# A two-layer transformer on one core: the maxima, totals, sums and biases around a feed-forward step are placed anew

## The chip, the cores and the metric

The kernel runs on one core of one Trainium2 chip. Its engines each work through a stream of their own: TensorE (PE in the profile; its weight loads are PEld), VectorE (DVE), ScalarE (ACT), GpSimd (POOL) and SyncE (SP), which here only issues DMAs. The metric is device time in microseconds (us) from the first to the last instruction of the core, median of several runs; less is better.

## The reference

Two transformer layers run one after the other over four sequences of 1024 tokens of width 512. Cut to what matters:

```python
# layer 0, 16 heads of 32, rotary positions
h = layer_norm(x) * (1 + scale1) + shift1          # shift, scale from cond
q, k, v = h @ wq + bq, h @ wk + bk, h @ wv + bv
q, k = rotary(q), rotary(k)
x = x + softmax(q @ k.T / sqrt(32) masked) @ v @ wo + bo
h = layer_norm(x) * (1 + scale2) + shift2
x = x + gelu(h @ ff_w1 + ff_b1) @ ff_w2 + ff_b2    # 512 -> 2048 -> 512
# layer 1: 16 query heads on 4 key/value heads, no positions, no mask
h = ln(x) * (1 + sc1) + sh1
x = x + g1 * (softmax(q @ k.T / sqrt(32)) @ v @ wo.T)
h = ln(x) * (1 + sc2) + sh2
x = x + g2 * (gelu(h @ w1.T + b1) @ w2.T + b2)
```

The result is float32. The kernel keeps it so by writing each operand of a product as a high and a low float16 half, and making three float16 products of the halves.

## The kernel before

**Images.** The work is eight images, `i` = 0 to 7: the four sequences of layer 0 (`i` = 0 to 3), then those of layer 1 (4 to 7). An image is an attention stage and a feed-forward stage. Every engine has an `attention(i)` and a `forward(i)`, written out by hand in one order, so each engine is a queue: a wait holds all that stands behind it. Semaphores (`Count` objects) link the queues.

**Attention.** It has 64 steps `s`. In each, TensorE makes four score tiles (128 keys x 512 queries, `score`, L946) into three PSUM banks in turn. ScalarE takes the exponential of each (`exps`, L1125) into `probs`, six units of two tiles in turn. TensorE multiplies a unit pair with the values (`values`, L963, bank 4). GpSimd adds two units (`add_probs`, L692) into `sums`, which TensorE multiplies by ones for the softmax denominators (`totals`, L978, bank 5): 64 additions `m`, and 32 totals, one for each pair of additions. A unit of `probs` is used again only when both its product and its addition are done. The eight last additions alternate between GpSimd and VectorE (`by_vector`: m = 57, 59, 61, 63).

Row maxima are needed before the exponential. For the next block of four heads TensorE makes scores a second time, with queries on the partitions (`max_item`, L884), and VectorE reduces each tile to a column (`tensor_reduce`, L1443). These tiles, and all other narrow work ("keys": projections `q`, `k`, `v`; output projection `wo`; transposes `ln1`, `ln2` of the normalised rows), go through three PSUM banks in attention and two (6 and 7) in the feed-forward stage; `bank_free` waits until the bank's reader is done. `fills_of` and `narrow_forward` say at which step which key stands. `wo` tiles 0 to 3 stand at steps 54 to 57 (`WO_AT`), their normalisation (`norm_apply`, L1343) right behind tile 3, the transposes at 61 and 62 (`LN2_AT`). Then come the last total, the feed-forward stage, and ScalarE's copies of bank 4 and 5 (`o_copy`, `d_copy`), VectorE's reciprocal of the last denominators (`invert_last`, L1460) and GpSimd's product of the two (`normalise`).

In layer 0 `k` and `q` are turned (rotary): VectorE makes four products in `turn`, GpSimd joins them (`rotate`, L677), ScalarE takes the high half, GpSimd the low half (`stack_low`, L682), SyncE puts them into the stack `ks` by six DMAs (`put_stack`, L518). `TURNS` holds the additions m behind which GpSimd does this. In images 0 to 3 weights are also split into halves (`split_low`, L1491), 18 chunks in image 0 and 7 each in images 1 to 3.

**Feed-forward.** Steps `n` = 0 to 32. At step n TensorE makes the first product of hidden chunk n (12 matmuls, L783 to L785 with `aT,ring`, into bank 4 or 5), then the second product of chunk n-1 (12 matmuls, three for each of four row tiles, `ring,probs`, banks 0 to 3), then the keys of that step. ScalarE takes the Gelu of chunk n into `g32` (L1271), VectorE splits it into halves (`split`, L1534 and L1535) and then drains the keys. Chunks 0 to 15 belong to the first 512 tokens, 16 to 31 to the others. At the end of each half VectorE reads the four row tiles (`output`, L1548 in layer 0, L1544 in layer 1). In layer 1 a second addition follows (`output_sum`, L1553). Keys of a feed-forward stage are the `wo` tiles 4 to 7 (n = 2, 3), transposes (n = 4 to 9), the next image's projections (n = 10 to 21), and its first 32 maxima, four each at n = 21 and 22 and three each at n = 23 to 30.

**GpSimd between them.** Behind the last addition it makes three deviations (L670, L672: reciprocal roots for normalisation) and adds the bias of the second product to all eight row tiles (`add_last_bias`, L711).

```python
                    for key in narrow_forward(i, n):      # TensorE, end of a forward step
                        narrow(key)
```

## Time and profile before

| | |
|---|---|
| median of 3 runs | 4138.36 us (4135.44 to 4140.47) |
| the profiled execution | 4144.66 us, its span 4142.9 us |
| TensorE busy | 3823.0 us, 92% |
| VectorE busy | 2498.1 us, 60% |
| GpSimd busy | 1626.7 us, 39% |
| ScalarE busy | 1605.7 us, 39% |
| granted TensorE clock, mean | 0.968 |

A layer-0 image takes some 537 us, a layer-1 image some 478 us, and images of a layer are alike almost to 0.1 us, step by step. So one image can be read closely and multiplied. Since all queues are in a fixed order, the question at each place is which wait of TensorE ends last, and what the engine that ends it did before.

### The profile page before, as it was taken

The numbers are of one execution on the slowest core, as the hardware profiler recorded it, in microseconds if no ns is written. First come the engines' busy times: TensorE is split into PE (matmuls) and PEld (weight loads), VectorE is DVE, ScalarE is ACT, GpSimd is POOL, SyncE is SP. The second block draws the span as 40 slices with busy tenths as digits, with TensorE's granted clock in tenths as the row PEclk, the third lists the DMA queues.
The fourth block names the chain that finished last, engine by engine and source line by source line (L and its number), as shares of the span: only waits on it lengthen the run. The fifth ranks groups of instructions, "written<-read, shape, count | busy, mean of one in ns | idle before, by whom it ended". The sixth has DMA issues, their size and how long they took to land.

```text
span 4142.9 us, 53495 instructions
## 1 busy us (share of the span) xinstructions
PE 3823.0 (92%) x20400; PEld 1511.9 (36%) x20400; DVE 2498.1 (60%) x3944; ACT 1605.7 (39%) x2807; POOL 1626.7 (39%) x907
## 2 busy tenths in 40 slices
PE   6898998998998989889899998999899998989999
PEld 4322443233533334333343333433244333433244
DVE  4687635767356764466654777367664776457752
ACT  1366312553125631155421663136521563126621
POOL 2377212673116742066510673026510573106620
PEclk9899999999999999999999999999999999999999
DMA  5233242221422223332222021311222112311112
GB/s 147 43 105 115 73 109 68 81 58 64 105 72 77 58 80 86 90 77 60 87 95 89 14 70 60 109 37 27 80 72 94 29 37 77 105 56 24 60 63 93
DMA packets 138973, 305.21 MB, mean 74 GB/s; under 512 B 19632, under 2 KB 59588, under 8 KB 137824
## 3 DMA queue, kind: packets, MB, share of 16 engines
q10 hardware_dynamic: 50944, 174.62, 13.0%
q1 hardware_dynamic: 87776, 127.17, 11.8%
q8 instruction: 164, 2.69, 0.3%
q14 instruction: 89, 0.73, 0.1%
HBM read 223.46 MB, written 36.66 MB: 63 GB/s over the span
## 4 chain that ended last, share of the span: by engine, by line
PE 76%; DVE 13%; issue 4%; POOL 3%; ACT 2%; DMA 1%; SPq 0%; ACTq 0%; DVEq 0%; POOLq 0%
PE ps L783 11%; PE ps L785 11%; PE ps L784 11%; PE ps L963 10%; PE ps L884 9%; PE ps L946 8%; PE ps L820 7%; PE ps L978 5%; DVE mcol L1443 3%; PE ps L837 2%; ACT probs L1125 2%; DVE turn L1365 1%; POOL sums L692 1%; DVE v_sb L1343 1%; PE ps L801 1%
## 5 line engine op out<-in xcount | busy, mean ns | idle before, releaser
L692 POOL TENSOR_TENSOR sums<-probs 128x1024 f32<-128x1024 f32 x480 | 1137.2, 2384 | 1393.0 <-ACT probs L1125 849.8
L1443 DVE TENSOR_REDUCE mcol<-ps 128x1 f32<-128x512 f32 x2048 | 1281.0, 683 | 368.5 <-PE ps L884 365.8
L1125 ACT ACTIVATE probs<-ps 128x512 f32<-128x512 f32 x2048 | 1100.5, 606 | 852.5 <-PE ps L946 625.9
L884 PE MATMUL ps<-ks,qs 97*128 97x512 f16 x2048 | 796.3, 395 | 126.2 <-DVE mcol L1443 76.0
L946 PE MATMUL ps<-qs,ks 98*128 98x512 f16 x2048 | 780.2, 392 | 78.0 <-ACT probs L1125 76.1
L1271 ACT ACTIVATE sums<-ps,cols 128x512 f32<-128x512 f32 x256 | 175.9, 687 | 1185.5 <-PE ps L785 1185.5
L963 PE MATMUL ps<-probs,v_sb 128*32 128x512 f32 x4096 | 560.1, 621 | 0.0
L884 PEld LDWEIGHTS ps<-ks,qs 97*128 97x128 f16 x2048 | 202.4, 99 | 708.2 <-DVE mcol L1443 436.1
L1534 DVE CAST probs<-sums 128x512 f16<-128x512 f32 x256 | 129.8, 507 | 485.7 <-ACT sums L1271 485.4
L783 PE MATMUL ps<-aT,ring 128*128 128x512 f16 x1024 | 395.2, 386 | 0.0
L784 PE MATMUL ps<-aT,ring 128*128 128x512 f16 x1024 | 394.0, 385 | 0.0
L785 PE MATMUL ps<-aT,ring 128*128 128x512 f16 x1024 | 393.7, 385 | 0.0
L783 PE MATMUL ps<-ring,probs 128*128 128x512 f16 x1024 | 388.6, 379 | 2.6 <-DVE probs L1535 2.5
L784 PE MATMUL ps<-ring,probs 128*128 128x512 f16 x1024 | 388.5, 379 | 0.0
L785 PE MATMUL ps<-ring,probs 128*128 128x512 f16 x1024 | 388.5, 379 | 0.0
L946 PEld LDWEIGHTS ps<-qs,ks 98*128 98x128 f16 x2048 | 198.8, 99 | 376.3 <-ACT probs L1125 245.8
L820 PE MATMUL ps<-hT,wqkv 128*128 128x512 f16 x1248 | 300.6, 386 | 4.8 <-DVE wqkv L1610 4.8
L978 PE MATMUL ps<-sums,ones 128*32 128x512 f32 x2048 | 277.6, 615 | 19.5 <-DVE sums L1436 19.5
L677 POOL TENSOR_TENSOR turn<-turn 128x512 f32<-128x512 f32 x32 | 41.6, 1299 | 610.4 <-DVE turn L1379 610.4
L1535 DVE TENSOR_TENSOR probs<-sums,probs 128x512 f16<-128x512 f32 x256 | 189.2, 739 | 8.8
L1379 DVE SCALAR_TENSOR_TENSOR turn<-ps,bias,trig 128x512 f32<-128x512 f32 x128 | 89.9, 746 | 166.5 <-PE ps L820 150.1
L820 PEld LDWEIGHTS ps<-hT,wqkv 128*128 128x128 f16 x1248 | 121.5, 99 | 164.3 <-issue 14.5
(107 smaller groups left out, 3286.5 us busy)
## 6 DMA issues: line engine op xcount, KB each, us to landing
ring<-halves ACTq DMA_DIRECT2D x208, 512.0 KB, 3.4
qs<-hl SPq DMA_DIRECT2D x192, 128.0 KB, 4.0
ring<-halves SPq DMA_DIRECT2D x48, 512.0 KB, 6.2
ring<-in_weights ACTq DMA_DIRECT2D x39, 512.0 KB, 4.3
halves<-ring ACTq DMA_DIRECT2D x37, 512.0 KB, 2.9
ks<-hl SPq DMA_DIRECT2D x120, 128.0 KB, 4.3
dcopy<-inverses SPq DMA_DIRECT2D x56, 256.0 KB
probs<-in_x SPq DMA_DIRECT2D x8, 1024.0 KB, 7.2
```

What stands on the lines that cost most here:

```text
L692: pool.tensor_tensor(sums[:, m % SUM_SLOTS, :, :], prob(u - 2), prob(u), ALU.add).then_inc(sum_set[0].sem, 1)
L783: pe.matmul(dst, lhs[0], rhs[0], start=first, stop=False)
L784: pe.matmul(dst, lhs[0], rhs[1], start=False, stop=False)
L785: return pe.matmul(dst, lhs[1], rhs[0], start=False, stop=last)
L820: mm = pe.matmul(bank, qkv(lw, weight_at(kind, i, hh, part, c), P), hT[:, lx, c, tok], start=(q == 0), stop=(q == 11))
L884: pe.matmul(bank, qs[0:K_MAX, hh, h, P * qt:P * qt + P], ks[0:K_MAX, key_set(i, hh), key_head(i, hh, h), 512 * half:512 * half + 512], sta ...
L946: pe.matmul(ps[:, bank, :], ks[0:K_EXP, key_set(i, hh), key_head(i, hh, h), P * kt:P * kt + P], qs[0:K_EXP, hh, h, :], start=True, stop=Tr ...
L963: mm = pe.matmul(ps[32 * q:32 * q + 32, 4, :], values_of(i, hh)[:, kt, value_cut(i, hh, 4 * g + q)], prob(u + q // 2)[:, q % 2, :], start= ...
L978: mm = pe.matmul(ps[32 * q:32 * q + 32, 5, :], ones32[:, :], sums[:, (m + q // 2) % SUM_SLOTS, q % 2, :], start=(m % 8 == 0), stop=(m % 8 ...
L1125: act.activation(prob(u)[:, e, :], ps[:, w % SCORE_BANKS, :], ACT.Exp).then_inc(exp_done.sem, 1)
L1443: dve.tensor_reduce(mcol[:, blk % 2, 4 * j + qt, half:half + 1], src, AX.X, ALU.max).then_inc(n_free[0], 1)
L1535: dve.tensor_tensor(fT[:, n % 4, 1, :], g32[:, n % 2, :], fT[:, n % 4, 0, :], ALU.subtract).then_inc(f_set.sem, 1)
```

## The change

- `forward` of TensorE: where a step's keys begin with a maximum and are more than two (`spread`), the first stands behind the first product, the second behind the second row tile of the second product, the rest at the end. VectorE takes the first maximum ahead of `split`.
- `totals`: the pair before the last comes one step later (behind the last `values`), the last pair behind the first product of the feed-forward stage. `d_copy(i, 7)` follows the first Gelu. `g32` moves to another slot of `sums`, so that the first Gelu waits for one total less. In layer 0 the first two pairs come one step earlier.
- `by_vector`: additions 57 and 59 go to GpSimd. `WO_AT`, `LN2_AT` are 2 less, `BIAS_AT` is earlier, the deviation stands at m = 53. `TURNS` of the second `k` half: low half at m = 3, high half at unit 10, its stack DMAs at step 6 ahead of the row DMA.
- `add_last_bias` waits until VectorE has applied the last normalisation of the next image.
- `output_sum` goes from VectorE to GpSimd: row tiles 0 to 3 behind the biases and builds, 4 to 7 behind additions 0 to 3 of the next image.
- `output` waits for each row tile by a new semaphore `y_full`, not for the whole product.
- `norm_apply` subtracts and multiplies in one instruction for each tile; the small instruction L1336 (`nm`) is gone.
- `split_low` is cut into two halves, at steps st and st+1.

```diff
-LAG, LAG_D = 4, 6
+LAG = 4
-WO_AT = 54
-LN2_AT = 61
-BIAS_AT = (50, 51, 52, 53, 54, 55, 56, 58)
+WO_AT = 52
+LN2_AT = 59
+BIAS_AT = (49, 49, 50, 51, 53, 54, 55, 56)
-("k", 1, 1), 3, 4, 11
+("k", 1, 1), 3, 3, 10
...
+def totals_step(i, pair):
+    return 2 * pair + (3 if layer(i) == 0 and pair < 2 else 4)
 def by_vector(m):
-    return m >= SUMS - 8 and m % 2 == 1
+    return m in (SUMS - 3, SUMS - 1)
+def spread(keys):
+    return len(keys) > 2 and keys[0][0] == "max"
...
             def output_sum(i, tt):                            # GpSimd
+                pool.wait_ge(y_read.sem, y_read.at(i, tt + 1))
+                pool.tensor_tensor(x1(i)[:, tt, :], x1(i)[:, tt, :], turn[:, tt % 4, :], ALU.add).then_inc(y_set.sem, 1)
...
+                    if gated(i - 1) and m < 4:
+                        output_sum(i - 1, 4 + m)
...
+                if i + 1 < NB:
+                    pool.wait_ge(ln_n, NORMS["ln1", i + 1, 1] + 1)
                 add_last_bias(i, 0)
...
-                    m = sum_of(max(u - LAG_D, 0))
-                    if u >= LAG_D and u - LAG_D == sum_unit(m):
-                        totals(i, m)
+                    if s == STEPS + 1:
+                        totals(i, SUMS - 4)
+                    for pair in range(SUMS // 2 - 2):
+                        if s == totals_step(i, pair):
+                            totals(i, 2 * pair)
...
                         mm.then_inc(f1_mm.sem, 1)
+                    if n == 0:
+                        totals(i, SUMS - 2)
+                    keys = narrow_forward(i, n)
+                    some(keys[0:1] if spread(keys) else ())
...
+                            if g == FC - 1 and t < 3:
+                                mm.then_inc(y_full.sem, 1)
+                            if t == 1:
+                                some(keys[1:2] if spread(keys) else ())
                         mm.then_inc(f2_mm.sem, 1)
-                    for key in narrow_forward(i, n):
-                        narrow(key)
+                    some(keys[2:] if spread(keys) else keys)
...
-                link(dve.scalar_tensor_tensor(out=nm[:, :], in0=mv[:, :, 0], scalar=-1.0, in1=rs[:, :],
-                                              op0=ALU.mult, op1=ALU.mult))
...
-                    last = dve.tensor_scalar(dst[:, t, :], src, rs[:, t:t + 1], nm[:, t:t + 1], ALU.mult, ALU.add)
+                    last = dve.tensor_scalar(dst[:, t, :], src, mv[:, t, 0:1], rs[:, t:t + 1], ALU.subtract, ALU.mult)
...
             def output(i, th):
-                dve.wait_ge(f2_mm.sem, f2_mm.at(i, FC * (th + 1)))
                 dve.wait_ge(xy_set.sem, xy_set.at(i, 4 * th + 4))
...
+                    if t < 3:
+                        dve.wait_ge(y_full.sem, y_full.at(i, 3 * th + t + 1))
+                    else:
+                        dve.wait_ge(f2_mm.sem, f2_mm.at(i, FC * (th + 1)))
...
                 for n in range(2 * FC + 1):
+                    keys = narrow_forward(i, n)
+                    for key in keys[0:1] if spread(keys) else ():
+                        narrow(key)
                     if n < 2 * FC:
                         split(i, n)
```

TensorE's order in image 0, from the last scores into the first product, before (L963 values, L978 totals, L783 to L785 the first product):

```order
L963 MATMUL ps<-probs,v_sb 32x512 x4
L978 MATMUL ps<-sums,ones 32x512 x4
L946 MATMUL ps<-qs,ks 128x512 x4
L963 MATMUL ps<-probs,v_sb 32x512 x8
L978 MATMUL ps<-sums,ones 32x512 x4
L963 MATMUL ps<-probs,v_sb 32x512 x4
L978 MATMUL ps<-sums,ones 32x512 x4
L783 MATMUL ps<-aT,ring 128x512
```

And now, where values are L986, totals L1001 and the first product L806 to L808 (its twelve matmuls are shown from the first and up to the last):

```order
L1001 MATMUL ps<-sums,ones 32x512 x4
L969 MATMUL ps<-qs,ks 128x512 x4
L986 MATMUL ps<-probs,v_sb 32x512 x12
L1001 MATMUL ps<-sums,ones 32x512 x4
L806 MATMUL ps<-aT,ring 128x512
...
L808 MATMUL ps<-aT,ring 128x512
L1001 MATMUL ps<-sums,ones 32x512 x4
L806 MATMUL ps<-aT,ring 128x512
```

The last total has moved behind the first product, and the one before it behind all values.

TensorE's order at the end of forward step 23 before: the second product's last row tile, three maxima (L884), and the next step:

```order
L783 MATMUL ps<-ring,probs 128x512
L784 MATMUL ps<-ring,probs 128x512
L785 MATMUL ps<-ring,probs 128x512
L884 MATMUL ps<-ks,qs 128x512 x3
L783 MATMUL ps<-aT,ring 128x512
```

The same stretch now (maxima L907):

```order
L808 MATMUL ps<-aT,ring 128x512
L907 MATMUL ps<-ks,qs 128x512
L806 MATMUL ps<-ring,probs 128x512
L807 MATMUL ps<-ring,probs 128x512
L808 MATMUL ps<-ring,probs 128x512
L806 MATMUL ps<-ring,probs 128x512
L807 MATMUL ps<-ring,probs 128x512
L808 MATMUL ps<-ring,probs 128x512
L907 MATMUL ps<-ks,qs 128x512
```

Each maximum now has six or more other matmuls between it and the next.

GpSimd's order in the same image, before, from the deviation at m = 55 to the biases between the stages (additions L692, bias L700, normalise L719, low half L725):

```order
L670 TENSOR_TENSOR sd<-mv,eps 128x4 [waits ln_var]
L672 TENSOR_TENSOR rs<-sd,eps 128x4 [waits sd_set]
L692 TENSOR_TENSOR sums<-probs 128x1024 [waits d_mul,exp_done]
L700 TENSOR_TENSOR ks<-ks,row_bc 128x512
L725 TENSOR_TENSOR aT<-ocopy,aT 128x512 [waits at_hi]
L692 TENSOR_TENSOR sums<-probs 128x1024 [waits d_mul,exp_done]
L700 TENSOR_TENSOR ks<-ks,row_bc 128x512
L692 TENSOR_TENSOR sums<-probs 128x1024 [waits d_mul,exp_done] x2
```

And now from the deviation at m = 53 (additions L702, bias L710, normalise L734, low half L740):

```order
L682 TENSOR_TENSOR rs<-sd,eps 128x4 [waits sd_set]
L702 TENSOR_TENSOR sums<-probs 128x1024 [waits d_mul,exp_done]
L710 TENSOR_TENSOR ks<-ks,row_bc 128x512
L734 TENSOR_TENSOR ocopy<-ocopy,dcopy 128x512 [waits inv_set,o_out]
L702 TENSOR_TENSOR sums<-probs 128x1024 [waits d_mul,exp_done]
L710 TENSOR_TENSOR ks<-ks,row_bc 128x512
L702 TENSOR_TENSOR sums<-probs 128x1024 [waits d_mul,exp_done]
L710 TENSOR_TENSOR ks<-ks,row_bc 128x512
L702 TENSOR_TENSOR sums<-probs 128x1024 [waits d_mul,exp_done]
L740 TENSOR_TENSOR aT<-ocopy,aT 128x512 [waits at_hi]
L702 TENSOR_TENSOR sums<-probs 128x1024 [waits d_mul,exp_done] x4
```

Behind the deviation GpSimd has eight additions where it had four.

## Rows read from the trace of the kernel before

**Rows 1.** Windows: stretch, its length, busy us per engine, granted clock, DMA share, GB/s.
```profile
1147.83:1200.43 52.60, 48.04 (x217) 20.88 (x216) 24.05 (x41) 5.50 (x8) 0.00 (x0) 1.00 0.15 50
4085.86:4127.30 41.44, 41.44 (x193) 18.75 (x192) 8.96 (x16) 5.50 (x8) 0.00 (x0) 1.00 0.20 68
1000.76:1018.92 18.16, 18.16 (x98) 9.75 (x97) 16.14 (x34) 5.19 (x8) 5.59 (x7) 1.00 0.27 87
1018.92:1038.87 19.95, 14.79 (x66) 7.45 (x64) 16.27 (x19) 4.37 (x7) 8.26 (x6) 0.83 0.15 53
910.51:977.45 66.94, 55.61 (x326) 18.33 (x324) 40.39 (x49) 35.49 (x64) 39.87 (x25) 0.95 0.23 82
3415.41:3482.98 67.57, 56.17 (x326) 18.44 (x324) 43.20 (x53) 34.63 (x63) 31.16 (x18) 0.95 0.24 84
2272.89:2290.75 17.86, 17.86 (x89) 5.08 (x88) 15.68 (x26) 12.97 (x24) 9.85 (x5) 0.90 0.24 75
2748.03:2770.05 22.02, 19.63 (x89) 5.49 (x88) 20.65 (x30) 13.38 (x24) 10.30 (x5) 0.85 0.24 72
```

**Rows 2.** TensorE's timeline, forward step 23: start, us, work [idle before, releaser].
```profile
1154.18 0.39 PE L884 MATMUL ps<-ks,qs 97*128 97x512 f16 x1 [0.57 <-DVE mcol L1443]
```

**Rows 3.** Timelines of GpSimd, VectorE and TensorE, forward steps 6 and 7, image 1.
```profile
1015.71 11.46 POOL L711 TENSOR_TENSOR ks<-ks,row_bc 128x512 f32<-128x512 f32 x8
...
1017.45 1.49 DVE L1534 CAST probs<-sums 128x512 f16<-128x512 f32 x1
...
1021.80 5.67 DVE L1343 TENSOR_SCALAR probs<-probs,rs,nm 128x512 f32<-128x512 f32 x4
...
1030.27 0.42 DVE L1534 CAST probs<-sums 128x512 f16<-128x512 f32 x1
...
1029.06 1.09 PE L801 MATMUL ps<-ident,v_sb 128*128 128x128 f32 x4 [4.79 <-DVE aT L1366]
```

**Rows 4.** Timelines of VectorE, TensorE and GpSimd, attention steps 58 to 60, image 1.
```profile
940.40 2.33 DVE L1336 SCALAR_TENSOR_TENSOR nm<-mv,rs 128x4 f32<-128x4 f32 x1 [1.41 <-POOL rs L672]
942.77 6.63 DVE L1343 TENSOR_SCALAR v_sb<-ks,rs,nm 128x512 f32<-128x512 f32 x4
949.33 1.21 DVE L1436 TENSOR_TENSOR sums<-probs 128x1024 f32<-128x1024 f32 x1
...
951.31 1.58 PE L946 MATMUL ps<-qs,ks 98*128 98x512 f16 x3 [6.12 <-ACT probs L1125]
...
942.67 1.27 POOL L700 TENSOR_TENSOR ks<-ks,row_bc 128x512 f32<-128x512 f32 x1
```

**Rows 5.** Timelines of TensorE, ScalarE and VectorE, end of attention, image 1.
```profile
971.26 1.07 PE L978 MATMUL ps<-sums,ones 128*32 128x512 f32 x8 [2.44 <-DVE sums L1436]
...
972.38 0.60 ACT L1137 ACTIVATE dcopy<-ps 128x512 f32<-128x512 f32 x1 [2.90 <-PE ps L978]
...
973.01 3.35 DVE L1460 RECIPROCAL dcopy<-dcopy 128x512 f32<-128x512 f32 x1 [1.90 <-ACT dcopy L1137]
```

**Rows 6.** Timelines of VectorE and TensorE, end of image 1's feed-forward stage.
```profile
1209.28 2.48 DVE L1548 SCALAR_TENSOR_TENSOR ks<-ps,ks 128x512 f32<-128x512 f32 x4 [1.85 <-PE ps L785]
...
1211.91 0.59 PE L884 MATMUL ps<-ks,qs 97*128 97x512 f16 x1 [2.23 <-DVE ks L1548]
```

**Rows 7.** VectorE's timeline, attention step 3, image 5.
```profile
2758.37 0.68 DVE L1553 TENSOR_TENSOR ks<-ks,turn 128x512 f32<-128x512 f32 x1
```

**Rows 8.** Timelines of GpSimd and TensorE, attention steps 5 to 8, image 2.
```profile
1242.55 2.35 POOL L692 TENSOR_TENSOR sums<-probs 128x1024 f32<-128x1024 f32 x1 [6.32 <-PE ps L978]
...
1261.21 0.58 PE L884 MATMUL ps<-ks,qs 97*128 97x512 f16 x1 [4.97 <-DMA ks<-hl]
```

**Rows 9.** VectorE's timeline, step 21, image 2; then line L1491: min/median/max ns.
```profile
1324.61 3.17 DVE L1491 SCALAR_TENSOR_TENSOR ring<-ring 128x1024 f16<-128x1024 f32 x1
...
L1491 DVE SCALAR_TENSOR_TENSOR ring<-ring x37: 1149/1224/3169, 190.7 to 1860.8; 128x1024 f16<-128x1024 f32 x37
```

**Rows 10.** GpSimd's timeline, steps 21 and 22, image 2: two additions.
```profile
1322.02 4.67 POOL L692 TENSOR_TENSOR sums<-probs 128x1024 f32<-128x1024 f32 x2 [1.23 <-PE ps L978]
```

More of the change, by code:

```diff
@@ L360, in program @@
         f2_mm = count("f2_mm", 2 * FC)
+        y_full = count("y_full", 6)
         exp_done = count("exp_done", SCORES)
@@ L733, in attention @@
                         add_probs(i, m)
-                    if layer(i) == 0 and m in BIAS_AT:
-                        add_bias(i, BIAS_AT.index(m))
-                    if m == 55:
+                    for tt, at_ in enumerate(BIAS_AT):
+                        if layer(i) == 0 and m == at_:
+                            add_bias(i, tt)
+                    if m == 53:
                         deviation("ln2", i, 0)
@@ L776, in _ @@
                     first_builds(i + 1)
+                if gated(i):
+                    for tt in range(4 if i + 1 < NB else NT):
+                        output_sum(i, tt)
         @block.tensor
@@ L982, in attention @@
             def attention(i):
-                for s in range(STEPS + LAG_D // 2):
+                for s in range(STEPS + LAG // 2):
                     u = 2 * s
@@ L1252, in attention @@
                 o_copy(i, 7)
-                d_copy(i, 7)
             def narrow(key):
@@ L1568, in forward @@
                             norm_apply("ln1", j, n // 6)
-                    for key in narrow_forward(i, n):
+                    for key in keys[1:] if spread(keys) else keys:
                         narrow(key)
```

42 lines of the change are left out of this document (22 added, 20 removed).

## Prediction

> **What bounds the kernel.** TensorE is busy 92% of the span, so it is the bound and only its waits and idle stretches can be gained. I read the timeline of one image of each layer step by step, noted where a step is longer than its matmuls, and put windows around those places [rows 1]. Feed-forward: in the last image, which has no next image's maxima, eight steps of 24 matmuls take 41.44 us, 0.216 us a matmul; in the others the same eight steps with three maxima each take 52.60. The 24 maxima themselves are 5.2, so 6.0 us are waits, three quarters of a microsecond a step: the third maximum waits until VectorE has read the first, as only two banks serve them [rows 2]. Steps 7 and 8 take 19.95 us where steps 4 to 6 take 6.05 each: GpSimd adds eight biases, VectorE's ops beside them stretch, and TensorE waits 4.79 us for a bank [rows 3]. The end of attention (from step 52 to the first matmul of the second product) takes 66.94 us in layer 0 and 67.57 in layer 1 [rows 1]; in it TensorE waits 6.12 us because VectorE is held in a normalisation ahead of addition 57 [rows 4], and 2.44 us for addition 63 [rows 5].
>
> The granted clock shows 0.83 and 0.95 in these windows against 1.00 around them: TensorE runs on its half level (1.2 of 2.4 GHz) for some us after such an idle stretch. So a removed wait can give back more than itself.
>
> **Part 1, spread maxima.** Now the first product, half a second product and the other half lie between maxima, 1.3 us or more, and VectorE takes the first maximum before Gelu is ready. Its work in a step, three maxima and two split ops, is half of the step (24.05 us of 52.60 [rows 1]), and the split is due a whole product later. So the waits go: 6.0 us for steps 23 to 30, and another 0.75 for step 22. Step 21 begins with a maximum only where the next image is of layer 1, 0.75 more in four of seven stages. 7 x 6.75 + 4 x 0.75 = **50 us**. Bounds: 4.6 us a stage (eight waits of 0.57 [rows 2]), so 32; and 55, if four maxima waited longer than three.
>
> **Part 2, biases behind the normalisation.** Steps 7 and 8 are 7.85 us over 2 x 6.05. The cast that takes 1.49 us beside GpSimd takes 0.42 alone [rows 3], a tensor op of the split's size 0.68 [rows 7]. So from 1017.45 on VectorE needs 0.42 + 0.7 for the split and, at the cast's length (an estimate), four times 0.46 for the applications, and is through near 1020.4 instead of 1027.5. Then GpSimd starts its eight biases, 1.27 each [rows 4], near 1020.5 to 1031, beside five VectorE ops on SBUF that each wait for one. Walking it through, TensorE waits 0.3 + 0.7 + 0.9 + 0.7 + 0.3 = 2.9 us in steps 7 to 9. Gain 7.85 - 2.9 = 5.0, seven times: **35 us**. Bounds: nothing (the same eight biases stand in another place) and 7.85 each, 55.
>
> How the two engines stand in each other's way is shown by one split op: it begins at 1324.61, takes 3.17 us where the median is 1.22 [rows 9], and GpSimd's second of two additions ran until 1326.69 [rows 10]. The op waits for the whole rest of that addition.
>
> The Trainium skill says this of the pair: one SBUF port pair is shared, whoever starts first keeps it for a whole instruction (SBUF — State Buffer, "SBUF: two separate sides"). The trace agrees, as above. It also advises against elementwise work on GpSimd, at about twice VectorE's time (GPSIMD Engine Reference, "4.1 Engine selection"); the trace agrees here too, 1.27 [rows 4] against 0.68 [rows 7]. By that rule parts 3 and 5 are steps in the wrong direction; what they do here is worked out in their own terms.
>
> **Part 3, end of attention.** VectorE no longer has addition 57 behind its normalisation (6.63 us [rows 4], where the small op ahead of it, 2.33, goes as well). But GpSimd now has: behind the deviation, additions 54 to 60 (7 x 2.34 [rows 10]), biases 3 x 1.27, and two ops of a bias's size: 23 us for layer 0, 19 for layer 1 (no biases there), and the exponentials of the last units wait for them. The `wo` tiles, 2.6 us each, move into steps 52 and 53 and out of 56 and 57, where they lengthen the stage no more. The walk, for image 1: step 56 begins at 933.7 (910.5 plus four steps of 6.3, 5.4, 6.9, 4.6), the deviation is done 1.9 later, addition 54 at 938, 55 at 943 (a bias and a normalise between), 57 at 950, 59 at 957, each on an exponential's path; unit 123 ends near 959, the total of step 62 and addition 61 near 963.4, the last two exponentials, the last values and bank 4's copy near 966.2. There the first product starts. In layer 1, without biases, the same walk ends 3.1 sooner. That is 6.1 us earlier in layer 0 (972.3 before) and 9.2 in layer 1. Some is given back: the last total now follows the first product (2.6 us), and behind it stand, as before, the copy of 0.60, the reciprocal of 3.35 [rows 5] and the split of 1.1 [rows 3, 7], for which the second product waits. So that starts 8.9 us behind the first, not 5.2 to 6. Net 2.4 in layer 0, 6.3 in layer 1: 4 x 8.7 = **35 us**. The copy cannot be late for the first product, as bank 4's copy runs under the last pair's total. Bounds: -3.7 an image (only the give-back; -30) and +7 in layer 0, +9 in layer 1 (GpSimd never late; 64).
>
> **Part 4, output by row tiles.** The four reads take 2.48 us, all behind the product, and TensorE idles 2.23 [rows 6]. Now three of them run under the product's last tiles, as far as VectorE has drained the two maxima before: 1.8 us earlier, seven times, **13 us**, and about 1 at the kernel's end, where the last sums, though slower on GpSimd, start sooner. Bounds 5 and 20 (the half clock at the next image's start gone too).
>
> **Part 5, output sums on GpSimd.** Images 5 to 7 spend 22.02 us on steps 0 to 5 where image 4, without output sums, takes 17.86 [rows 1]. GpSimd's pair of 2.34 + 1.27 = 3.6 us a step for four steps is above the 3 us of a step there, so I give back half: 3 x 2.1 = **6 us**. Bounds -6 (queue never catches up) and 12.5.
>
> **Part 6, the second key half of layer 0.** Addition 3 waits 6.32 us for the first total, and TensorE 4.97 for the stack's DMAs three steps later [rows 8]. With totals one step earlier and the low half right behind the turn, the six DMAs go out some 5 us sooner. I count 4.5 of the wait, and 1.5 of the half clock behind it: 4 x 6 = **24 us**. The row DMA is now queued behind the six on SyncE; it is needed a step later, and if late takes 2 us of this back. Bounds 10 and 28.
>
> **Part 7, halved split op.** 39 of them. GpSimd's pairs of additions fill the odd steps, so one half of each now falls into a free step and one into a busy one. Those that cost 3.17 cost about 2.6 and 0.6, and those that were free (1.22 in even steps) now meet an addition: **0**. Bounds -20 and +15.
>
> **The sum.** 50 + 35 + 35 + 13 + 1 + 6 + 24 + 0 = 164 us. The profiled execution took 4144.7 and would take 3980.7; the median is 6.3 below it, so 3974 us.
>
> **Rivals.**
> *Contention pays it back.* GpSimd is queued wherever work was taken from VectorE: parts 2 and 3 come to nothing. For it: 23 us of GpSimd work in a row on the path. Against: those waits had VectorE behind GpSimd twice over. 4144.7 - 94 - 6.3 = 4044. Chance 0.13.
> *Maxima not freed.* The first maximum now stands ahead of the split on VectorE and the spread ones meet its ops, so the wait moves to the second product: part 1 gives nothing, 4024. Against it speaks VectorE's half-empty step. Chance 0.05.
> *Everything clears, the clock too.* All upper bounds but part 7's: 55 + 55 + 64 + 21 + 12 + 28 = 235, so 3903. For it: each wait is tied to a stretch at half clock, and a shorter chain tends to unlock the next. Chance 0.16.
> *Slower: the halved splits.* Twice as many VectorE ops meet an addition of up to 2.34 us while holding the maxima, and ScalarE, which stores the split and is in order, now waits for the later half. If each of 39 costs 5 us, 195 are lost: 4144.7 - 164 + 195 - 6.3 = 4169. It decides from 4.2 us a split; today's worst step loses about that, but only seven splits meet it. Chance 0.02.
>
> **How the numbers follow.** The forecast has the remaining 0.64; its own range from the bounds is 3930 to 4030. Most of the second case and of the clearing one must be within: low 3925, high 4045. 0.2% is about what a measurement of this kernel can tell from no change. Only the last rival is slower: 0.02; within 0.2% 0.01; faster 0.97.
>
> **What would show it.** Forward steps 23 to 30 in 46.6 us; steps 7 and 8 near 15 without an idle stretch of 4 us; no wait above 1 us for the stack's DMAs at attention step 7; TensorE's idle before the next image's first maximum below 0.7; between first and second product near 9 us, with the reciprocal as the last releaser. If GpSimd is the releaser of long waits of ScalarE in steps 56 to 60, part 3 was right in kind. A wait of the second product for the split in steps 22 to 30, or of ScalarE's queue for the halved split, would prove me wrong.

## The result, and the profile after

The changed kernel takes 4037.31 us (median of four runs, 4033.12 to 4039.97); the kernel before, on the same chip, 4139.41 (also of four). One run of the kernel before, 4235.98 us, lies apart in a slower state and is left out of the ratio, whose other three runs have a median of 4138.36. The ratio is 0.9755, 95% interval 0.9738 to 0.9772. So it is faster, by 102 us where 164 were forecast; 4037 lies inside the range 3925 to 4045, near its upper end. The profiled execution's span is 4038.1 us against 4142.9, so the two traces hold the whole difference.

Windows of the changed kernel, with the columns of [rows 1] and in the same order of places:

```profile
1128.80:1175.53 46.73, 46.73 (x218) 21.05 (x216) 24.65 (x41) 5.50 (x8) 0.00 (x0) 1.00 0.19 62
3982.41:4023.85 41.44, 41.44 (x193) 18.78 (x192) 8.96 (x16) 5.50 (x8) 0.00 (x0) 1.00 0.20 67
990.70:1008.86 18.16, 18.16 (x98) 9.77 (x97) 15.95 (x36) 5.19 (x8) 2.41 (x4) 1.00 0.26 87
1008.86:1020.96 12.10, 12.10 (x66) 6.51 (x64) 11.93 (x14) 4.26 (x7) 10.80 (x7) 1.00 0.27 88
893.97:965.76 71.79, 59.35 (x325) 18.93 (x324) 37.05 (x47) 36.77 (x66) 46.44 (x28) 0.90 0.23 82
3320.89:3393.74 72.85, 60.34 (x326) 18.59 (x324) 41.13 (x51) 35.42 (x64) 36.68 (x20) 0.91 0.22 80
2210.93:2228.36 17.43, 16.91 (x90) 4.68 (x89) 15.46 (x26) 12.95 (x24) 9.86 (x5) 1.00 0.31 76
2672.31:2690.00 17.69, 17.10 (x89) 4.52 (x88) 15.45 (x26) 12.49 (x23) 12.83 (x7) 1.00 0.21 75
```

Read against [rows 1], line by line: the eight forward steps with maxima fall from 52.60 to 46.73, steps 7 and 8 from 19.95 to 12.10, and in both TensorE is now busy without a gap. Steps 0 to 5 of image 5 fall from 22.02 to 17.69. But the end of attention became longer: from step 52 to the second product 71.79 us and not 66.94 in image 1, 72.85 and not 67.57 in image 6, at a granted clock of 0.90 and not 0.95.

I cut both traces at the same matmuls and summed over the eight images. This is the table that the rest is about (us saved, minus is lost):

| stretch | part | forecast | measured |
|---|---|---|---|
| forward steps 21 to 30 | 1, spread maxima | 50 | 53.4 |
| forward steps 7 to 9 | 2, biases later | 35 | 56.8 |
| attention step 52 to first product | 3, end of attention | | -7.7 |
| first to second product | 3, last total | | -31.1 |
| second product to forward step 4 | 3 | | -6.5 |
| all of part 3 | 3 | 35 | -45.3 |
| end of the second product to the next image, and kernel's end | 4, output by tile | 14 | 14.3 |
| attention steps 0 to 6 | 5, output sums | 6 | 10.0 |
| attention steps 7 and 8 | 6, second key half | 24 | 30.0 |
| attention steps 9 to 51 | 7, halved split | 0 | -15.0 |

With 0.3 from forward steps 4 to 6 the sum is 104.5, of a difference of 104.8 between the spans.

The places where it went well, in the changed kernel's timelines (VectorE, TensorE and GpSimd of image 1) and in one line of TensorE's waits:

```profile
1008.17 1.91 DVE L1374 TENSOR_SCALAR probs<-probs,mv,rs 128x512 f32<-128x512 f32 x4
...
1013.58 1.49 DVE L1571 CAST probs<-sums 128x512 f16<-128x512 f32 x1
...
1182.51 2.56 DVE L1590 SCALAR_TENSOR_TENSOR ks<-ps,ks 128x512 f32<-128x512 f32 x4
...
1185.21 0.38 PE L907 MATMUL ps<-ks,qs 97*128 97x512 f16 x1 [0.44 <-DVE ks L1590]
...
1010.16 12.47 POOL L721 TENSOR_TENSOR ks<-ks,row_bc 128x512 f32<-128x512 f32 x8 [4.48 <-DVE probs L1374]
...
PE ps L907 <- DMA ks<-hl: 0.3, 1, 0.3
```

The application of the norm takes 1.91 us for four tiles where it took 5.67 beside GpSimd [rows 3], and the eight biases begin only behind it. TensorE's wait for the last output is 0.44, not 2.23 [rows 6], and of the waits for the stack's DMAs (4.97 in [rows 8]) 0.3 us is left in the whole kernel.

Where it went badly, GpSimd, VectorE and TensorE of the changed kernel at steps 56 to 61 of image 6:

```profile
3346.99 0.20 POOL L680 TENSOR_TENSOR sd<-mv,eps 128x4 f32<-128x4 f32 x1 [4.50 <-DVE mv L1364]
...
3348.26 2.35 POOL L702 TENSOR_TENSOR sums<-probs 128x1024 f32<-128x1024 f32 x1
...
3351.98 5.01 POOL L702 TENSOR_TENSOR sums<-probs 128x1024 f32<-128x1024 f32 x2
3361.10 2.36 POOL L702 TENSOR_TENSOR sums<-probs 128x1024 f32<-128x1024 f32 x1 [4.10 <-PE ps L1001]
...
3364.53 2.35 POOL L702 TENSOR_TENSOR sums<-probs 128x1024 f32<-128x1024 f32 x1
3372.36 4.97 POOL L702 TENSOR_TENSOR sums<-probs 128x1024 f32<-128x1024 f32 x2 [5.49 <-PE ps L1001]
...
3348.32 8.96 DVE L1374 TENSOR_SCALAR v_sb<-ks,mv,rs 128x512 f32<-128x512 f32 x4 [1.41 <-POOL rs L682]
...
3367.57 0.63 PE L824 MATMUL ps<-ident,v_sb 128*128 128x128 f32 x4 [2.38 <-DVE aT L1397]
```

These additions are m = 54, then 55 and 56, 57, 58, then 59 and 60. GpSimd first waits 4.50 us for VectorE's statistics, with addition 54 queued behind. Then VectorE's four applications take 8.96 us beside its additions (1.91 above, alone). Additions 57 and 59 wait 4.10 and 5.49 us for totals: only three slots hold sums, so an addition needs the total of the one three before it, and that total stands in TensorE's queue behind score tiles, values and transposes.

And between the two products, VectorE and TensorE of the same image:

```profile
3388.38 3.35 DVE L1493 RECIPROCAL dcopy<-dcopy 128x512 f32<-128x512 f32 x1 [3.03 <-ACT dcopy L1169]
...
3392.05 1.64 DVE L1572 TENSOR_TENSOR probs<-sums,probs 128x512 f16<-128x512 f32 x1
...
3388.49 0.38 PE L806 MATMUL ps<-aT,ring 128*128 128x512 f16 x1 [0.81 <-ACT dcopy L1169]
3393.74 0.39 PE L806 MATMUL ps<-ring,probs 128*128 128x512 f16 x1 [2.50 <-DVE probs L1572]
```

The second product begins 9.8 us behind the first, waiting for the split, which waits for the reciprocal, which waits for the copy of the last total.

### The profile page after: what moved, and what is told of

Read it like the earlier page. It is cut to its first block, busy times and chain, and to the rows that moved or that the text cites. A ratio compares the mean times of both kernels' runs of the same rounds, so it can differ in the third digit from the quotient of the medians.

```text
span 4038.1 us, 53506 instructions
## 1 busy us (share of the span) xinstructions
PE 3800.2 (94%) x20400; PEld 1502.4 (37%) x20400; DVE 2466.3 (61%) x3903; ACT 1603.3 (40%) x2807; POOL 1711.6 (42%) x955
## 4 chain that ended last, share of the span: by engine, by line
PE 80%; DVE 9%; POOL 4%; issue 3%; ACT 3%; DMA 1%; SPq 0%; ACTq 0%; POOLq 0%; DVEq 0%
PE ps L806 12%; PE ps L807 12%; PE ps L808 12%; PE ps L986 10%; PE ps L907 9%; PE ps L969 8%; PE ps L843 7%; PE ps L1001 5%; DVE mcol L1476 3%; PE ps L860 2%; POOL sums L702 2%; ACT probs L1157 2%; DVE ring L1526 2%; PE ps L824 1%; DVE dcopy L1493 1%
## 5 line engine op out<-in xcount | busy, mean ns | idle before, releaser
L702 POOL TENSOR_TENSOR sums<-probs 128x1024 f32<-128x1024 f32 x496 | 1175.6, 2384 | 1039.5 <-PE ps L1001 570.0
L907 PE MATMUL ps<-ks,qs 97*128 97x512 f16 x2048 | 790.6, 388 | 64.4 <-DVE mcol L1476 47.0
L986 PE MATMUL ps<-probs,v_sb 128*32 128x512 f32 x4096 | 568.0, 631 | 0.0
L907 PEld LDWEIGHTS ps<-ks,qs 97*128 97x128 f16 x2048 | 199.7, 98 | 624.9 <-DVE mcol L1476 375.2
L806 PE MATMUL ps<-ring,probs 128*128 128x512 f16 x1024 | 390.8, 382 | 20.6 <-DVE probs L1572 20.6
L806 PE MATMUL ps<-aT,ring 128*128 128x512 f16 x1024 | 388.3, 379 | 6.5 <-ACT dcopy L1169 6.5
L808 PE MATMUL ps<-ring,probs 128*128 128x512 f16 x1024 | 389.9, 381 | 0.0
L807 PE MATMUL ps<-aT,ring 128*128 128x512 f16 x1024 | 388.2, 379 | 0.0
L808 PE MATMUL ps<-aT,ring 128*128 128x512 f16 x1024 | 388.0, 379 | 0.0
L1001 PE MATMUL ps<-sums,ones 128*32 128x512 f32 x2048 | 280.6, 621 | 0.0
L1572 DVE TENSOR_TENSOR probs<-sums,probs 128x512 f16<-128x512 f32 x256 | 207.4, 810 | 8.8
```

The source lines that it names most:

```text
L702: pool.tensor_tensor(sums[:, m % SUM_SLOTS, :, :], prob(u - 2), prob(u), ALU.add).then_inc(sum_set[0].sem, 1)
L806: pe.matmul(dst, lhs[0], rhs[0], start=first, stop=False)
L807: pe.matmul(dst, lhs[0], rhs[1], start=False, stop=False)
L808: return pe.matmul(dst, lhs[1], rhs[0], start=False, stop=last)
L907: pe.matmul(bank, qs[0:K_MAX, hh, h, P * qt:P * qt + P], ks[0:K_MAX, key_set(i, hh), key_head(i, hh, h), 512 * half:512 * half + 512], sta ...
L986: mm = pe.matmul(ps[32 * q:32 * q + 32, 4, :], values_of(i, hh)[:, kt, value_cut(i, hh, 4 * g + q)], prob(u + q // 2)[:, q % 2, :], start= ...
```

## The experiments

Each kernel is the changed one, or the one before, with the edit shown. Differences "by the traces" are from the same cuts as in the table. The runs are from several chips, so each ratio is to the kernel before as measured beside that run, and kernels are best compared by their ratios.

### Transposes back to steps 61 and 62 (r_ln2)

```diff
-LN2_AT = 59
+LN2_AT = 61
```

> The changed kernel, LN2_AT back to 61: the transposes of the second normalisation stand at steps 61 and 62 again, all else stays. In the changed kernel TensorE waits 2.5 us at step 60 for VectorE's low half of the first pair of transposes, and its totals, which free the slots of the sums, stand behind them; GpSimd's next addition waits 6.4 us (image 1) and 8.3 us (image 6) for such a total. Theory A (TensorE's order: the earlier transposes are what ate the gain): the stall of step 60 goes, the stretch from step 52 to the first product becomes 4 to 6 us shorter in each of eight images, 4037 - 32 to 48 = 3989 to 4005. Theory B (GpSimd's queue, longer by additions 57 and 59, is what ate it): this edit changes less than 1 us an image, 4029 to 4045. A transposition that then stands right ahead of the first product may cost up to 2 us an image under either.

Measured: 4039.92 us, ratio 0.9752 (0.9737 to 0.9766), the same as the changed kernel. Step 60 of image 6 falls from 7.98 to 3.65 us as theory A wanted, but step 62 grows from 4.43 to 7.37 and step 63 from 4.99 to 6.25. TensorE, GpSimd and VectorE of this kernel there:

```profile
3372.07 1.09 PE L824 MATMUL ps<-ident,v_sb 128*128 128x128 f32 x4 [1.60 <-DVE aT L1397]
...
3378.07 2.37 POOL L702 TENSOR_TENSOR sums<-probs 128x1024 f32<-128x1024 f32 x1 [6.88 <-ACT probs L1157]
...
3378.67 2.32 DVE L1397 TENSOR_TENSOR aT<-turn,aT 128x512 f16<-128x512 f32 x1
```

The wait goes with the transposes. Over eight images the stretch to the first product is 6.2 us shorter, and 3.2 of it are lost behind. Theory A falls as the cause. Theory B is left standing, without being shown yet.

### Additions 57 and 59 back on VectorE (r_vec)

```diff
-    return m in (SUMS - 3, SUMS - 1)
+    return m >= SUMS - 8 and m % 2 == 1
```

> The changed kernel, by_vector as before: additions 57, 59, 61, 63 on VectorE. Theory B (GpSimd's queue ate the gain): step 52 to the first product becomes 3 to 6 us shorter an image, 3989 to 4013. Theory A (TensorE's order): VectorE's norm_lo ops now have two more additions of 1.2 us beside them and the first of them stands behind the normalisation again, 0 to 3 us longer an image, 4037 to 4061.

Measured: 4014.67 us, ratio 0.9693 (0.9677 to 0.9709). The stretch to the first product is 31.1 us shorter by the traces, 2.9 to 4.5 in each image, 3.9 on average, where theory B asked 3 to 6. The whole kernel gains less, some 23 us, and so ends 2 us above theory B's 4013: 5.5 us are lost in steps 9 to 51, which the edit doesn't touch, and 1.7 behind the second product. Theory B holds for the stretch, at its lower end. VectorE, GpSimd and TensorE in steps 59 to 61 of image 6 (additions 57 to 60):

```profile
3343.20 1.23 DVE L1469 TENSOR_TENSOR sums<-probs 128x1024 f32<-128x1024 f32 x1 [3.78 <-PE ps L1001]
...
3351.52 1.23 DVE L1469 TENSOR_TENSOR sums<-probs 128x1024 f32<-128x1024 f32 x1 [1.75 <-PE ps L1001]
...
3345.29 2.36 POOL L702 TENSOR_TENSOR sums<-probs 128x1024 f32<-128x1024 f32 x1 [3.18 <-ACT probs L1157]
...
3352.90 2.36 POOL L702 TENSOR_TENSOR sums<-probs 128x1024 f32<-128x1024 f32 x1 [5.25 <-ACT probs L1157]
...
3348.47 0.63 PE L824 MATMUL ps<-ident,v_sb 128*128 128x128 f32 x4 [0.93 <-DVE aT L1397]
```

Both additions that go back take 1.23 us and not 2.36, and 59 and 60 no longer stand in a row (4.97). The feared loss, that the first of them would again stand behind the normalisation, isn't there: the normalisation was over before addition 57's slot was free. GpSimd now waits for exponentials, and not they for it. What this run can't separate is the longer addition itself from its meetings with VectorE's low halves of the transposes. The one that takes 1.61 us in the changed kernel takes 0.69 here, but a later one takes 2.30.

### The last total in front of the first product (r_total)

```diff
-                    if n == 0:
-                        totals(i, SUMS - 2)
...
+                totals(i, SUMS - 2)
...
                 o_copy(i, 7)
+                d_copy(i, 7)
...
-                    if n == 0:
-                        d_copy(i, 7)
```

On TensorE the last total stands behind the last step of attention, on ScalarE its copy behind that of bank 4.

> The changed kernel with the last pair's total in front of the first product of the feed-forward stage again, and the copy of bank 5 ahead of the first Gelu, as in the kernel before. Theory C1 (the total costs what it delays: copy, reciprocal and split run beside the first product again, but TensorE waits for addition 63, 1.4 us, and makes the total, 1.0, before it): first product 2.6 us later, second product 5.8 behind it and not 9.8, net 1.4 us an image, 4037 - 11 = 4026. Theory C2 (my prediction's reading: the whole give-back of 3.7 us an image is the price of the move): 4037 - 30 = 4007. If the move had been a gain, the time is above 4040.

Measured: 4024.76 us, ratio 0.9713 (0.9697 to 0.9729). Its span is 4023.5 us, 14.6 less than the changed kernel's. The first product comes later by 17.3 us in sum, the second follows it 32.4 sooner, and 6.5 more come from a stretch that is at half clock in four images of the changed kernel. TensorE waits 1.51 us for addition 63, as C1 said, and 0.65 for the split:

```profile
3375.57 1.06 PE L1001 MATMUL ps<-sums,ones 128*32 128x512 f32 x8 [1.51 <-DVE sums L1467]
...
3382.57 0.39 PE L806 MATMUL ps<-ring,probs 128*128 128x512 f16 x1 [0.65 <-DVE probs L1570]
```

These three make 21.5; 7.1 of it are lost again in steps 9 to 51 of the layer-0 images, which the edit doesn't touch. So moving the total costs some 15 us net in this order of work, up to 21 if that loss is chance: C1, above its 11. The 31 us between the products are not its price; 17 of them are bought back by the earlier first product.

### The reciprocal behind the first split (r_recip)

```diff
-                invert_last(i)
...
                 dve.wait_ge(gelu_done.sem, gelu_done.at(i, n + 1))
+                if n == 0:
+                    dve.wait_ge(*sum_done(SUMS - 2, i))
...
+                    if n == 0:
+                        invert_last(i)
```

All on VectorE: `invert_last` goes from the end of `attention` to behind `split(i, 0)`. The new wait for addition 62 takes over what the reciprocal's own wait had covered: the split writes where that addition reads.

> The changed kernel, with VectorE's last reciprocal (3.35 us) behind the first split of the feed-forward stage, not ahead of it. Theory C (the give-back of some 4 us an image between first and second product is the chain last total, copy, reciprocal, split, which now begins behind the first product): the second product starts near 5.3 us behind the first, not 9.8, so 8 x 4.5 = 36 us less, 4001. If the wait were for the Gelu or its table load (1.28 us) instead, 9.8 would fall to 8 or more and the time to 4023 at best. The reciprocal could delay the second split; it has about 5 us to the third product.

Measured: 4016.67 us, ratio 0.9695 (0.968 to 0.9709). The second product starts 7.1 us behind the first (21.6 us in sum) and the half-clock stretch behind it is gone (6.5). VectorE and TensorE, image 6:

```profile
3370.01 0.69 DVE L1573 TENSOR_TENSOR probs<-sums,probs 128x512 f16<-128x512 f32 x1
3370.62 3.34 DVE L1493 RECIPROCAL dcopy<-dcopy 128x512 f32<-128x512 f32 x1
...
3370.59 0.38 PE L806 MATMUL ps<-aT,ring 128*128 128x512 f16 x1 [0.81 <-ACT dcopy L1169]
```

Theory C is right in kind, its size (4001) wasn't: I had left out TensorE's own queue. Between the two products stand the total (1.04), the wait of 0.81 for its copy and another first product (2.6), so 7.1 and not 5.3 is the floor.

### The weight split in one piece (r_split)

```diff
                         if s == st:
-                            split_low(i, q, 0)
-                        if s == st + 1:
-                            split_low(i, q, 1)
+                            split_low(i, q)
```

`split_low` is again the one op of 1024 elements of the kernel before.

> The changed kernel with the weight split in one piece again (39 ops instead of 78). The stage sums of the two traces put the loss of steps 9 to 52 at 15 us; theory D (the halves cause it): 4037 - 15 = 4022, steps 9 to 24 and 24 to 52 as in the kernel before. Rival: the loss comes from the totals that stand two units earlier in TensorE's order there, and the halves cost nothing: 4037 within 3.

Measured: 4018.06 us, ratio 0.9695 (0.9679 to 0.9712), 20.2 us by the traces: theory D, and more than it asked. The line of the split op in the changed kernel (min/median/max ns, first and last start), then the same in this kernel, then a half in the changed kernel's timeline of VectorE:

```profile
L1526 DVE SCALAR_TENSOR_TENSOR ring<-ring x74: 615/780/2752, 184.2 to 1815.4; 128x512 f16<-128x512 f32 x74
```

```profile
L1524 DVE SCALAR_TENSOR_TENSOR ring<-ring x37: 1149/1226/3164, 183.7 to 1788.7; 128x1024 f16<-128x1024 f32 x37
```

```profile
771.86 2.63 DVE L1526 SCALAR_TENSOR_TENSOR ring<-ring 128x512 f16<-128x512 f32 x1
```

A half that meets an addition takes 2.63 us, nearly as long as a whole (3.16). Together the halves keep VectorE busy for 98.0 us and the whole ones for 65.3: the same lines grouped by form show this.

```profile
L1526 DVE SCALAR_TENSOR_TENSOR ring<-ring 128x512 f16<-128x512 f32 x74 | 98.0, 1327 | 4.8 <-ACT ring L1183 4.8
```

```profile
L1524 DVE SCALAR_TENSOR_TENSOR ring<-ring 128x1024 f16<-128x1024 f32 x37 | 65.3, 1764 | 4.8 <-ACT ring L1183 4.8
```

VectorE's longer busy time is not yet a loss; the loss is where somebody waits. ScalarE issues the DMA that stores each split, in its own queue, two steps behind the first half, and the second half now stands one step later. One line of ScalarE's waits in the changed kernel (us in total, times, longest), and VectorE and ScalarE of image 0 at steps 56 and 57:

```profile
ACT probs L1157 <- DVE ring L1526: 24.4, 9, 10.5
```

```profile
399.11 7.85 DVE L1374 TENSOR_SCALAR v_sb<-ks,mv,rs 128x512 f32<-128x512 f32 x4 [1.41 <-POOL rs L682]
406.88 1.75 DVE L1526 SCALAR_TENSOR_TENSOR ring<-ring 128x512 f16<-128x512 f32 x1
...
409.11 3.05 ACT L1157 ACTIVATE probs<-ps 128x512 f32<-128x512 f32 x6 [10.46 <-DVE ring L1526]
```

Here the second half stands behind the normalisation on VectorE, and the exponentials behind the store on ScalarE, for 10.46 us. Neither the kernel before nor this one has any such wait. Six of the nine, 19.0 us, are in image 0, which has 18 of the 39 splits; 15.2 of the 15.8 us that this run gains in steps 9 to 51 are in image 0 too. Whether two short ops at one place, with the store where it was, would cost anything was not tried.

### The kernel before with the spread maxima alone (p_spread)

The edit is the lines with `spread` of the diff above, on TensorE and VectorE.

> The kernel before with the spread maxima alone (the order of the keys on TensorE and VectorE, nothing else). If the waits of steps 21 to 30 are that order's alone: step 21 to the end of step 30 shortens by 53 us over seven stages, 4139 - 53 = 4086. If the rest of the change had a part in it (outputs by tile, sums on GpSimd), less than 45, above 4094.

Measured: 4089.32 us, ratio 0.987 (0.9855 to 0.9885). Forward steps 21 to 30 are 53.4 us shorter (41.2 and 12.3), as in the changed kernel to a tenth, the other stretches of the images give 1 us back, and the start ahead of the first attention stage is 2 us shorter. Part 1 stands by itself.

### The kernel before with the later biases alone (p_bias)

```diff
                     deviation("ln1", i + 1, 1)
+                    pool.wait_ge(ln_n, NORMS["ln1", i + 1, 1] + 1)
                 add_last_bias(i, 0)
```

> The kernel before with one wait more: GpSimd adds the last biases only when VectorE has applied the next image's second normalisation. If their meeting was the whole cost of steps 7 and 8: 57 us over seven stages, 4139 - 57 = 4082, each of steps 7 to 9 in 6.05. If the shorter application of the changed kernel (one small instruction less, two scalars from one pair) had a part in it, up to 16 us of that stay missing: 4098.

Measured: 4092.87 us, ratio 0.9877 (0.9862 to 0.9892). Forward steps 7 to 9 are 56.5 us shorter; the attention stages give back 4. So the order of the two engines there was the whole cost, and the shorter application of the changed kernel had no part in it: one wait in one queue is worth 52 us.

### The kernel before with only the earlier places at the end of attention (p_end)

```diff
-WO_AT = 54
-LN2_AT = 61
-BIAS_AT = (50, 51, 52, 53, 54, 55, 56, 58)
+WO_AT = 52
+LN2_AT = 59
+BIAS_AT = (49, 49, 50, 51, 53, 54, 55, 56)
...
-                    if m == 55:
+                    if m == 53:
                         deviation("ln2", i, 0)
```

> The kernel before with only the earlier places at the end of attention: wo tiles at 52, transposes at 59, biases from 49, deviation at 53; additions and totals stay. In the runs of the changed kernel the placing is bound up with the totals (worth some 17 us there in that stretch, taken back behind it) and with additions 57 and 59 (-31). Theory E (the placing is worth nearly nothing, because the chain of deviation, additions, normalisation and transposes moves with it): step 52 to the first product shortens by 6 us over eight images, within 10 of it, 4139 - 6 = 4133. My prediction's reading (the placing is the gain, 6 to 9 us an image): 50 to 70 us, 4070 to 4090.

Measured: 4149.14 us, ratio 1.0008 (0.9998 to 1.0018): nothing. By the traces the first product comes earlier, by 17.3 us in sum (3.2 an image in layer 0, 1.1 in layer 1), and 18.6 and 7.1 are lost behind it. (The trace is of the fastest of ten runs; it also has 8.4 us less in steps 9 to 51, which the edit doesn't touch, and so its span is 4 us under the kernel before's.) GpSimd, ScalarE, VectorE and TensorE around the second product of image 6:

```profile
3465.01 1.26 POOL L719 TENSOR_TENSOR ocopy<-ocopy,dcopy 128x512 f32<-128x512 f32 x1 [3.16 <-DMA dcopy<-inverses]
...
3466.37 0.60 ACT L1138 ACTIVATE dcopy<-ps 128x512 f32<-128x512 f32 x1 [2.87 <-POOL ocopy L719]
...
3467.00 3.35 DVE L1461 RECIPROCAL dcopy<-dcopy 128x512 f32<-128x512 f32 x1 [3.66 <-ACT dcopy L1138]
...
3472.81 0.61 PE L784 MATMUL ps<-ring,probs 128*128 128x512 f16 x1 [2.95 <-DVE probs L1536]
```

A chain that was hidden is late next: the copy of the last denominators shares its buffer with block 6's, and must wait until GpSimd has used those, for which GpSimd waits for a DMA. A first product that comes earlier only waits longer behind itself. Theory E holds for the sum; for the stretch to the first product it said 6 and 17 came.

### Three edits together (combo1)

The edits of r_vec, r_recip and r_split in the changed kernel.

> The changed kernel with three edits of the first four runs together: additions 57 and 59 on VectorE again, the reciprocal behind the first split, the weight split in one piece. Alone they brought 23, 24 and 20 us by the stage sums (31, 28 and some 18 in the stretches that they touch). They act in different stretches, so they should add up: 4037 - 67 = 3970. If the reciprocal, one step nearer to the second split, is in the way of VectorE's additions, or the clock takes some back: up to 3985.

Measured: 3957.74 us, ratio 0.9551 (0.9537 to 0.9565). By the traces 81.5 us less than the changed kernel, where the three alone had 67.7. Of the 13.7 that are more, 3.1 lie in the stretch to the first product (36.5, where the three gave 31.1, 3.5 and -1.2), 3.1 behind the second product, where no image is at half clock any more, and 7.8 in steps 9 to 51, where r_vec and r_recip alone had lost some. The forecast of 3970 was too high by 12.

### The deviation one or two additions later (combo3, combo2, combo4)

```diff
-                    if m == 53:
+                    if m == 54:
                         deviation("ln2", i, 0)
```

combo3 is combo1 with this edit, m = 54:

> The kernel with the three edits together, and the deviation behind addition 54 and not 53. In it GpSimd waits 4.5 us in a layer-1 image for VectorE's statistics with addition 54 queued behind the wait. Theory F (that wait holds addition 54, and with it the exponentials of steps 57 and 58): addition 54 runs inside the wait, the stall of steps 57 and 58 (some 7 us with the clock) shortens by 2 us in layer 1 and by less than 1 in layer 0: 3958 - 10 = 3948. Rival: the normalisation comes later by what addition 54 takes, and the exponentials then wait beside it: 3958 or up to 8 more.

combo2 is combo1 with 55:

> As the run before this one, with the deviation behind addition 55, as in the kernel before. Theory F: additions 54 and 55 and the normalisation of block 6's values are ahead of the normalisation on VectorE, which starts 1 to 3 us later; the stall of step 58 goes, but addition 57 on VectorE and the transposes at step 59 wait for it: 3945 to 3965. Rival (VectorE's normalisation is the chain): 2 us an image longer than with 54, 3965 to 3980.

combo4 is combo2 with `LN2_AT = 61`:

> As the run before this one, with the transposes at 61 and 62 too: only the wo tiles stay two steps earlier. If the transposes at 59 wait for the late normalisation there, this is 1 to 3 us an image shorter, 3935 to 3955. If a transposition late in the stage costs its chain of 5 us wherever it stands, as the first run showed, no change within 5.

Measured: 3931.66 us for combo3, ratio 0.9488 (0.9474 to 0.9502); 3939.80 for combo2, 0.9508 (0.9494 to 0.9522); 3953.82 for combo4, 0.954 (0.9526 to 0.9554). GpSimd of image 6 in combo1, then in combo3:

```profile
3282.21 0.20 POOL L680 TENSOR_TENSOR sd<-mv,eps 128x4 f32<-128x4 f32 x1 [4.51 <-DVE mv L1364]
...
3283.48 2.35 POOL L702 TENSOR_TENSOR sums<-probs 128x1024 f32<-128x1024 f32 x1
```

```profile
3259.42 2.35 POOL L702 TENSOR_TENSOR sums<-probs 128x1024 f32<-128x1024 f32 x1 [0.17 <-ACT probs L1157]
3263.76 0.20 POOL L680 TENSOR_TENSOR sd<-mv,eps 128x4 f32<-128x4 f32 x1 [1.99 <-DVE mv L1364]
```

Addition 54 now runs inside the wait for the statistics, which shrinks from 4.51 to 1.99. The stretch to the first product is 22.8 us shorter in sum, twice what theory F said (its 3948 was 16 us too high). One reason is that the stall of steps 57 and 58 loses part of its half clock too (a granted clock of 0.55 in step 58 of image 6 before, 0.83 now). At 55 the time is again under theory F's range, by 5 us, but the order of the two is as it said: layer 1 stays within 1 us of combo3, layer 0, with its biases in the same queue, loses 3 us in three images. combo4 is worse than combo2 by 10.5 us there, against both of its theories: late transposes cost 1 to 2 us an image here, where in r_ln2 they gained 0.8; what makes the difference is not shown.

combo3 beats both kernels: 2.7% under the changed one by the ratios (0.9488 over 0.9755), 5.1% under the one before.

## Why the prediction was right, and where it wasn't

**Right in sign and range, and not by its middle.** The sum missed by 59 us: part 3 gave 80 less, part 7 gave 15 less, parts 2, 6, 5 and 1 gave 22, 6, 4 and 3 more. That the time is within the range at all is partly luck: without these 35 us it would be near 4072, and part 3 alone is 15 us below its own lower bound.

**Part 1** was right in kind and nearly in size: 53.4, with p_spread to show that it is the order alone. Its eight steps take 46.73 us; I had written 46.6.

**Part 2** failed by one term, the 2.9 us of waits in steps 7 to 9. The place of the application was right (it is over 1.3 us into step 7, I had 1.5), and VectorE's ops do stretch beside the biases (a cast of 1.49, VectorE busy for 11.93 of 12.10 us). But TensorE never waits. The biases still cost VectorE time and take it from nobody. The upper bound was the value, and a little more (56.8 for 55). p_bias shows that the order alone does it.

**Part 3, the step that failed** is the walk: "addition 54 at 938, 55 at 943 (a bias and a normalise between), 57 at 950, 59 at 957, each on an exponential's path ... There the first product starts. ... That is 6.1 us earlier in layer 0 (972.3 before) and 9.2 in layer 1." From the start of step 52 it put the first product at 55.7 us in image 1; it came at 62.0. Up to addition 58 the walk is good: it has addition 57 at 39.5 and the trace at 38.5. Addition 59 comes at 50.7 and not 46.5, since it waits 6.4 us for a total, as the row at 3372.36 above shows for image 6 (5.49); another 2 are lost in the last additions. The walk had GpSimd as a queue with a length. It is one member of a ring: addition, exponential, values, total, next addition, with transposes and the normalisation's split in TensorE's and VectorE's share of it. An engine in such a ring that takes twice as long for the same addition lengthens the turn, however little it is busy; this reading rests on the rows, and on r_vec for its size. r_vec showed 31 us in this stretch (23 in the whole kernel) for additions 57 and 59, combo3 another 23 for one addition behind a wait. The prediction's sign for this part did come: GpSimd releases ScalarE three times in steps 56 to 60 of image 1, 6.8 us in all, where it was once and 0.4 before. But the sign only says who holds ScalarE, and was no proof of a gain. The price of the placing itself, the wo tiles, transposes and biases, is nothing (p_end), where the forecast had its gain.

The Trainium skill has a rule on this, as quoted ahead of the result (GPSIMD Engine Reference, "4.1 Engine selection"): elementwise work belongs to VectorE. By it parts 3 and 5 were steps in the wrong direction. For part 3 the runs agree: 1.23 against 2.36 us, and 31 us in the stretch. For part 5 the trace speaks against it: steps 0 to 6 are 10 us shorter with the sums on GpSimd, where nothing in the ring waits for them. No run has tried that move alone.

**The give-back** was sized right: I said 8.9 us from first to second product with the reciprocal as releaser, 9.8 came. I erred on what stands against it. Without an earlier first product it is a plain loss; r_total puts the net of the move at 15 to 21 us.

**The rival "contention pays it back"** was half right: it had parts 2 and 3 come to nothing. Part 3 did, and went below by more than my lower bound (-45 against -30); part 2 went the other way. The rival "maxima not freed" had nothing for it. "Slower" was far off in its size (195 us, with 20 measured), but it had the right mechanism for part 7: ScalarE, which stores the split in order, waits for the later half.

**Part 4** (14.3 for 14) and **part 5** (10 for 6; GpSimd's queue did catch up, image 5 takes 17.69 us and needs no half back) stand in the trace alone. **Part 6** gave 30, above the bound of 28: all of the wait went, and its half clock. None of the three was tried by itself.

**Part 7** was argued from the right fact and summed wrongly: "Those that cost 3.17 cost about 2.6 and 0.6" and those that were free meet an addition. The first halves are right to the digit (2.63). But that is a loss: 2.6 + 0.6 is no less than 3.17, and every free one that becomes 0.6 + 2.6 adds 2. There was nothing on the other side of that sum, so 0 was no middle. Nor was VectorE's time the path by which it is paid: by the trace that was ScalarE's wait for the second half, 24.4 us in nine waits, which the prediction had named itself as what would prove it wrong. r_split says 20 us, at my lower bound.

## What to carry to other kernels

When an operation moves to an engine that is little busy, ask whether somebody waits for it within a ring of engines; if so, its longer duration is paid at each turn, and the engine's idle share says nothing. Before an op that waits is placed in a queue, let what is ready go first: one addition ahead of such a wait was worth 0.6% here. An op that stretched beside another engine's work gained nothing here by being halved; and if a queue waits for the last piece, that piece is now later, as ScalarE's exponentials showed, which stood behind it. And when a stage's start is moved forward, follow the next chain that isn't moved: in p_end a DMA kept the second product nearly where it was.

## What the runs showed of the hardware

**A VectorE op beside GpSimd pays for GpSimd's instruction, large or small.** Beside additions a split of 512 elements took 2.63 us (0.78 median) and one of 1024 took 3.16 (1.23 median); four applications took 8.96 us beside additions and 1.91 without. The Trainium skill says that the pair of ports is held for a whole instruction and the other engine blocks (SBUF — State Buffer, "SBUF: two separate sides"). The trace agrees for VectorE. GpSimd's own additions hardly grow: 5.01 us for the two beside the four applications, where twice 2.35 is 4.70. Its shorter biases grow more: eight beside VectorE's ops took 12.47, where eight times 1.27 is 10.2.

**The half clock does not follow from the wait alone.** The second product of image 1 and of image 6 both wait 2.50 us for the split. In image 1 its first matmul then takes 0.61 us (half clock), in image 6 it takes 0.39:

```profile
965.76 0.61 PE L806 MATMUL ps<-ring,probs 128*128 128x512 f16 x1 [2.50 <-DVE probs L1572]
```

Four of eight images pay 1.6 us for this in the changed kernel; in r_vec it is other images (0, 3, 5, 6 and 7 pay, 1 and 2 don't), in combo1 none. Attention stages also differ by 1.5 or 3 us between edits that don't touch them, and between images of one kernel: in the kernel before, steps 9 to 51 take 181.9, 178.5 and 176.8 us in images 1 to 3, so they are not as alike there as I wrote ahead of the prediction. What decides it stays open; it is why single stretches of steps 9 to 51 are not read closer than that here.
